# Five layer norms taken apart into blocks inside the neighbouring stages, with the root by Newton steps on VectorE

## The chip, the cores and the metric
The kernel runs on one core of one Trainium2 chip. The time is the device time of one execution in microseconds (us), lower is better.

## What is computed
The input x has 8 sequences of 256 tokens and 128 features. Five stages are added to it one after another, each behind a layer norm without scale and shift; the last two kinds of stage share their weights between calls.

```python
def _layernorm(x, axis=-1, eps=1e-05):
    m = jnp.mean(x, axis=axis, keepdims=True)
    v = jnp.var(x, axis=axis, keepdims=True)
    return (x - m) / jnp.sqrt(v + eps)
...
    x = x + 0.5 * _L0_ffn_ref(_layernorm(x, axis=-1), ...)    # mixture: router, 8 experts, top 2, and a shared one
    x = x + _L0_attn_ref(_layernorm(x, axis=-1), ...)         # four blocks of linear attention and MLP
    x = x + 0.5 * _L0_ffn_ref(_layernorm(x, axis=-1), ...)
    x = x + 0.5 * _L1_ffn_ref(_layernorm(x, axis=-1), ...)    # experts with a capacity: each takes its top 32 tokens of a sequence
    x = x + _L1_attn_ref(_layernorm(x, axis=-1), ...)         # causal attention, 16 heads of 8
    x = x + 0.5 * _L1_ffn_ref(_layernorm(x, axis=-1), ...)
    return x
```

## The kernel before
The state xr lies in SBUF with features on the 128 partitions and the 2048 tokens along the free axis, in four blocks (tb 0 to 3) of 512 tokens. The order on each engine is the order of the code; semaphores counted up by the producers tie the engines together. The stages are ffn0(0), attn0, ffn0(1), ffn1(0), attn1, ffn1(1).

A layer norm stands ahead of every stage but attn0, whose own first norm is part of its periods. It treats all four blocks at once between two stages (norm_parts, on TensorE from L479, on ScalarE from L1002, layer_norm and layer_norm_whole on VectorE from L1326). Per block: TensorE multiplies by the centring matrix into a PSUM bank (xc, L487), ScalarE squares (sq, L1005), TensorE averages over the partitions by a matrix of 1/128, so that each variance stands on all 128 partitions (var, L493), ScalarE takes Ln (L1009). When all four are done it loads another table and takes Exp of -0.5 times that (L1013), VectorE multiplies (L1329 or L1345). For three of the norms the result is also split into a rounded high half by ScalarE (high, L1017) and a low half by VectorE (low, L1334). Matmuls in which accuracy matters are made three times with these halves (mm3, L122 to L124).

The mixture, ffn0, has 72 units n. Unit n is up(n) on TensorE (six matmuls), gate(n) on ScalarE (silu), product(n) on VectorE, weigh(n) by the router's weight from unit 8 on, high(n) on ScalarE, the low half on GpSimd (L1800), and down(n) on TensorE four units later (LAG0). up(n) waits for product(n-2). Ahead of it stand the router's logits, 16 matmuls of 8 columns (L517). On VectorE, best() finds the two largest, places() their indices, choose() makes the weights; a DMA through DRAM spreads them. In the first call VectorE also splits four experts' weights between the products (split), and GpSimd four more (L1804). add(tb) adds a finished block to xr.

attn0 runs in 20 periods (PERIODS); period p works on block p mod 4 in its newest role and on three older roles. The last three periods only drain. In each, ScalarE's last gelu is fed (L1133), on which VectorE's residual2 (L1509) waits; behind that TensorE centres (L573), and so on to finish (L1513), which adds the block to xr.

ffn1 scores the tokens (L667), turns z (L672), picks 32 tokens per expert by eight rounds of max on VectorE, gathers, multiplies in 32 steps g, and at the end turns the outputs back (outputs), scales them by their gate on ScalarE (gated) and scatters them with one-hot matrices (scatter); add(tb) adds a block when two sequences are scattered. attn1 begins with project_in of block 0 in two halves (quad 0 and 1), each of four mm3; ScalarE (hm, L1248) and VectorE (stk, L1689) stack the results, and then the heads' scores follow (plain, L814). Its last steps are outputs, flip, normalise, turn, project_out and add.

## Time and profile before
| | us |
|---|---|
| median of 3 runs | 1147.11 |
| lowest and highest | 1139.55, 1149.39 |
| profiled execution | 1144.14 |
| its span | 1142.4 |
| TensorE, VectorE, ScalarE, GpSimd busy | 954.2, 672.9, 626.3, 349.1 |

The span is the part of the profiled execution in which instructions ran. Busy times overlap. In the rows below an engine's name is short: PE is TensorE, PEld its weight loads, DVE VectorE, ACT ScalarE, POOL GpSimd. A matmul of fp32 stands as two records, one of the halves as one.

### The profile page before, as it was taken

What the parts mean: (1) busy time and instruction counts of PE and PEld (TensorE: products, weight loads), DVE (VectorE), ACT (ScalarE), POOL (GpSimd) and SP (SyncE); (2) the same over time, 40 slices, a digit from 0 to 9 for tenths busy, and PEclk for the clock granted to TensorE, in tenths of its full rate; (3) what the DMA queues carried; (4) which work ended last, traced back from release to release, by engine and by line L of the source; (5) the groups of instructions that cost most, each with busy time, mean ns of one, the idle gap of its engine ahead of it and who ended that gap; (6) DMA issues with size and microseconds to landing.
All of it is one profiled execution on the core that took longest, in us unless ns stands there. A gap on an engine that the chain in (4) does not pass through costs nothing.

```text
span 1142.4 us, 12658 instructions
## 1 busy us (share of the span) xinstructions
PE 954.2 (84%) x4387; PEld 637.8 (56%) x4395; DVE 672.9 (59%) x1247; ACT 626.3 (55%) x986; POOL 349.1 (31%) x257
## 2 busy tenths in 40 slices
PE   6899997599999998689999974998567777675998
PEld 4678884233333333257888852886344554443797
DVE  2888885567777877437888826242645545226222
ACT  5455554378888887645555554445342544443443
...
DMA packets 30932, 33.61 MB, mean 29 GB/s; under 512 B 2254, under 2 KB 19990, under 8 KB 30870
## 3 DMA queue, kind: packets, MB, share of 16 engines
...
q14 instruction: 27, 0.22, 0.1%
...
## 4 chain that ended last, share of the span: by engine, by line
PE 63%; DVE 20%; ACT 10%; POOL 3%; issue 3%; DMA 0%; SPq 0%; ACTq 0%; DVEq 0%; POOLq 0%
PE ps L122 10%; PE ps L123 9%; PE ps L124 9%; PE ps L595 5%; PE ps L732 5%; DVE smax L1697 3%; PE ps L753 2%; PE ps L589 2%; PE ps L814 2%; PE ps L487 2%; PE ps L573 2%; ACT L1139 2%; ACT ex L1258 2%; PE ps L493 2%; PE ps L704 2%
## 5 line engine op out<-in xcount | busy, mean ns | idle before, releaser
L1800 POOL TENSOR_TENSOR fl<-fp,fh 128x512 fp32r<-128x512 f32 x144 | 225.6, 1588 | 128.5 <-ACT fh L1062 128.4
L1053 ACT ACTIVATE fs<-ps 128x512 f32<-128x512 f32 x144 | 86.2, 599 | 115.6 <-PE ps L124 115.3
L1396 DVE TENSOR_TENSOR fp<-fp,cwb 128x512 f32<-128x512 f32 x128 | 139.0, 1086 | 13.7 <-DVE fp L1389 0.5
L1389 DVE TENSOR_TENSOR fp<-fs,ps 128x512 f32<-128x512 f32 x144 | 98.1, 682 | 38.8 <-ACT fs L1053 37.6
L122 PE MATMUL ps<-z_hi,w_hi 128*128 128x512 f32 x288 | 116.7, 405 | 3.4 <-DVE fp L1389 3.3
L123 PE MATMUL ps<-z_lo,w_hi 128*128 128x512 f32 x288 | 115.7, 402 | 0.0
L124 PE MATMUL ps<-z_hi,w_lo 128*128 128x512 f32 x288 | 114.1, 396 | 0.0
L1062 ACT CAST fh<-fp 128x512 fp32r<-128x512 f32 x144 | 88.8, 617 | 34.7 <-DVE fp L1396 30.2
L1865 POOL TENSOR_TENSOR ln_sq<-ln_rs 128x512 f32<-128x512 f32 x20 | 21.1, 1056 | 272.8 <-ACT ln_rs L1102 272.8
L1858 POOL TENSOR_SCALAR_AFFINE_SELECT ex<-ex 128x1024 f32<-128x1024 f32 (+1 forms) x24 | 33.7, 1403 | 171.8 <-ACT ex L1258 171.8
L1697 DVE TENSOR_REDUCE smax<-ps 128x8 f32<-128x2048 f32 (+1 forms) x24 | 55.0, 2291 | 34.0 <-PE ps L828 27.3
L814 PE MATMUL ps<-stk 32*128 32x128 f32 (+1 forms) x512 | 34.3, 384 | 41.3 <-DVE smax L1697 15.6
L1198 ACT ACTIVATE hid<-ps 128x512 f32<-128x512 f32 x64 | 38.5, 601 | 52.8 <-PE ps L124 52.6
L122 PEld LDWEIGHTS ps<-z_hi,w_hi 128*128 128x128 f32 x288 | 55.6, 193 | 18.6 <-DVE fp L1389 5.9
L732 PE MATMUL ps<-hid,w 128*128 128x256 f32 x256 | 65.2, 379 | 0.0
L589 PE MATMUL ps<-z,wb 128*128 128x512 f32 x128 | 62.4, 614 | 2.7 <-DVE qq L1472 2.7
L124 PEld LDWEIGHTS ps<-z_hi,w_lo 128*128 128x128 f32 x288 | 55.5, 193 | 12.7
L122 PE MATMUL ps<-fh,w_hi 128*128 128x512 f32 x144 | 57.3, 398 | 5.8 <-POOL fl L1800 5.8
L123 PEld LDWEIGHTS ps<-z_lo,w_hi 128*128 128x128 f32 x288 | 55.7, 193 | 10.9
L1258 ACT ACTIVATE ex<-ps 128x2048 f32<-128x2048 f32 x24 | 44.8, 1872 | 29.1 <-PE ps L814 29.1
L595 PE MATMUL ps<-hid,wb 128*128 128x512 f32 x128 | 60.2, 593 | 0.0
L581 PE MATMUL ps<-z,wb 128*128 128x512 f32 x96 | 49.6, 657 | 10.7 <-DVE z L1447 10.7
...
## 6 DMA issues: line engine op xcount, KB each, us to landing
...
stk<-mT SPq DMA_DIRECT2D x64, 4.0 KB
```

The lines of the kernel that those rows point to most:

```text
L122: pe.matmul(out, w_hi, x_hi, start=start, stop=False)
L123: pe.matmul(out, w_hi, x_lo, start=False, stop=False)
L124: return pe.matmul(out, w_lo, x_hi, start=False, stop=stop)
L589: pe.matmul(ps[:, bank, :], wb[:, b, (4 + k) * P:(5 + k) * P], blk(z, t), start=True, stop=True).then_inc(a0_matmul[t], 1)
L595: pe.matmul(ps[:, A0_WO, :], wb[:, b, w], hid[:, k, :], start=(k == 0), stop=(k == FT - 1)).then_inc(a0_matmul[t], 1)
L732: ins = pe.matmul(ps[:, OUT1[n % 2], 0:SEQ], w2[:, e, ft * P:(ft + 1) * P], hid[:, g % RING1, f * SEQ:(f + 1) * SEQ], start=(ft == 0), sto ...
L1053: act.activation(fs[:, n % 2, :], ps[:, n % 2, :], ACT.Silu).then_inc(silu_done, 1)
L1062: act.copy(fh[:, n % RING0, :], fp[:, n % RING0, :]).then_inc(fhi_done, 1)
L1389: dve.tensor_tensor(f, fs[:, n % 2, :], ps[:, 2 + n % 2, :], ALU.mult).then_inc(prod_done, 1)
L1396: dve.tensor_tensor(f, f, cwb[:, x % CW_RING, :], ALU.mult).then_inc(weighed, 1)
L1697: dve.tensor_reduce(smax[:, s % 2, int(k > 0), :, hgs], ps[:, bank:bank + 4, :].rearrange("p g (h t) -> p g h t", h=HG if k == 0 else 2), ...
L1800: pool.tensor_tensor(fl[:, n % RING0, :], fp[:, n % RING0, :], f32(fh[:, n % RING0, :]), ALU.subtract).then_inc(flo_done, 1)
```

## The change
The norm is cut into six steps that are each called for one block: ln_centre, ln_variance and ln_spread on TensorE, ln_square and ln_high on ScalarE, ln_root, ln_scale and ln_low on VectorE. The old norm_parts, layer_norm and layer_norm_whole and the Ln and Exp with their table loads are gone. ln_square also copies the centred block to z, since the bank is written again. ln_variance has the squares as weights and one column of 1/128 as the moving side, so that each token's variance comes out once, in four columns on the partitions. ln_root makes the reciprocal root there, on 128x4 values: a seed by integer arithmetic and three Newton steps. ln_spread multiplies the identity by one column repeated 128 times, which puts the root of each token on every partition again. ln_scale multiplies that with z.

New steps on TensorE, with the banks:

```diff
-LG_BANK, CW_BANK = OUT0[0], OUT0[3]
+LG_BANK, CW_BANK = OUT0[1], OUT0[3]
...
+LN_BANK = {LN_FFN0: (4, 5, 6, 7), LN_FFN0B: (5, 5, 6, 7), LN_FFN1: OUT0, LN_ATTN1: (0, 1, 6, 7), LN_FFN1B: (0, 1, 3, 5)}
...
+def ln_centre(n, tb):
+    pe.wait_ge(ln_in, NTB * n + tb + 1)
+    pe.matmul(ps[:, LN_BANK[n][tb], :], centre[:], blk(xr, tb), start=True, stop=True).then_inc(xc_ready, 1)
+def ln_variance(n, tb):
+    pe.wait_ge(sq_ready, 2 * (NTB * n + tb + 1))
+    for q in range(TPB):
+        ins = pe.matmul(ps[:, LN_BANK[n][tb], q:q + 1], LN_SQ[n][:, tb, q * P:(q + 1) * P], mean_w[:, 0:1], start=True, stop=True)
+    ins.then_inc(var_ready, 1)
...
+def ln_spread(n, tb):
+    pe.wait_ge(rs_ready, NTB * n + tb + 1)
+    for q in range(TPB):
+        ins = pe.matmul(ps[:, LN_BANK[n][tb], q * P:(q + 1) * P], ln_r[:, tb, q:q + 1].broadcast_to([P, P]), ident[:],
+                        start=True, stop=True)
+    ins.then_inc(spread_ready, 1)
```

On ScalarE:

```diff
+def ln_square(n, tb):
+    act.wait_ge(xc_ready, NTB * n + tb + 1)
+    act.activation(LN_SQ[n][:, tb, :], ps[:, LN_BANK[n][tb], :], ACT.Square).then_inc(sq_ready, 1)
+    act.copy(blk(z, tb), ps[:, LN_BANK[n][tb], :]).then_inc(sq_ready, 1)
...
+def ln_high(n, tb):
+    act.wait_ge(y_done, NTB * HALVED.index(n) + tb + 1)
+    act.copy(blk(z_hi, tb), blk(z, tb)).then_inc(zh_done, 1)
```

On VectorE:

```diff
+def ln_root(n, first, last=None):
+    last = first if last is None else last
+    v, r, t = (x[:, first:last + 1, :] for x in (ln_v, ln_r, ln_t))
+    for tb in range(first, last + 1):
+        dve.wait_ge(var_ready, NTB * n + tb + 1)
+        own.did(dve.tensor_scalar(ln_v[:, tb, :], ps[:, LN_BANK[n][tb], 0:TPB], EPS_OUT, None, ALU.add))
+    own.wait()
+    own.did(dve.tensor_scalar(r.bitcast(I32), v.bitcast(I32), -0.5, ROOT_SEED, ALU.mult, ALU.add))
+    own.wait()
+    for step in range(ROOT_STEPS):
+        own.did(dve.tensor_tensor(t, r, r, ALU.mult))
+        own.wait()
+        own.did(dve.scalar_tensor_tensor(out=t, in0=t, scalar=-0.5, in1=v, op0=ALU.mult, op1=ALU.mult))
+        own.wait()
+        ins = dve.scalar_tensor_tensor(out=r, in0=t, scalar=1.5, in1=r, op0=ALU.add, op1=ALU.mult)
+        if step < ROOT_STEPS - 1:
+            own.did(ins)
+            own.wait()
+    ins.then_inc(rs_ready, last + 1 - first)
+def ln_scale(n, tb):
+    done = y_done if n in HALVED else z_ready
+    dve.wait_ge(spread_ready, NTB * n + tb + 1)
```

Where they are called. The start, on TensorE and then on VectorE:

```diff
+ln_centre(LN_FFN0, 1)
+ln_variance(LN_FFN0, 0)
+ln_centre(LN_FFN0, 2)
+ln_variance(LN_FFN0, 1)
+ln_spread(LN_FFN0, 0)
+ln_spread(LN_FFN0, 1)
+ln_variance(LN_FFN0, 2)
+ln_spread(LN_FFN0, 2)
 pe.wait_ge(par_loaded, 16 * (len(PAR_NAMES) + 6))
...
 dve.tensor_scalar(centre[:], ident[:], -1.0 / P, None, ALU.add).then_inc(centre_ready, 1)
 own.did(dve.tensor_copy(ident_b[:], ident[:]))
+ln_root(LN_FFN0, 0, 1)
+ln_scale(LN_FFN0, 0)
...
 dve.wait_ge(w0_loaded[0], 16 * W0_LOADS[0])
 halves(w0_hi[:, 0, :], w0_lo[:, 0, :], w0_raw[:, 0, :]).then_inc(w0_split, 1)
+ln_low(LN_FFN0, 0)
```

The mixture, on TensorE, ScalarE and VectorE; the norm of ffn1(0) begins inside the second call:

```diff
+    pe.wait_ge(z_ready, u0 + 1)
+    up(0)
+    ln_centre(ln, NTB - 1)
+    up(1)
+    logits(1)
     logits(0)
-    up(0)
-    for tb in range(1, NTB):
-        logits(tb)
-    for n in range(1, ALL0):
+    ln_variance(ln, NTB - 1)
+    logits(2)
+    up(2)
+    ln_spread(ln, NTB - 1)
+    up(3)
+    logits(3)
+    for n in range(4, ALL0):
         up(n)
-        if n >= LAG0:
-            down(n - LAG0)
...
+        down(n - LAG0)
+        if n == LAG0 + 2:
             weights()
+        if call == 1:
+            for tb in range(NTB - 1):
+                if n == LAST0[tb] + 8:
+                    ln_centre(LN_FFN1, tb)
+                if n == LAST0[tb] + 10:
+                    ln_variance(LN_FFN1, tb)
+                if n == LAST0[tb] + 13:
+                    ln_spread(LN_FFN1, tb)
+                if n == LAST0[tb] + 16:
+                    scores(LN_FFN1, tb)
     for n in range(ALL0 - LAG0, ALL0):
         down(n)
+    if call == 1:
+        ln_centre(LN_FFN1, NTB - 1)
+        ln_variance(LN_FFN1, NTB - 1)
+        ln_spread(LN_FFN1, NTB - 1)
+        scores(LN_FFN1, NTB - 1)
...
+            ln_square(ln, NTB - 1)
+            ln_high(ln, 2)
         if n >= 1:
             high(n - 1)
-        if n == LAG0 + 1:
+        if n == 3:
+            ln_high(ln, NTB - 1)
+            weigh_two()
+        if n == LAG0 + 2:
             weights()
...
+    ln_low(ln, 2)
     product(0)
+    ln_root(ln, NTB - 1)
+    product(1)
+    ln_scale(ln, NTB - 1)
+    product(2)
+    ln_low(ln, NTB - 1)
     best()
...
+        if call == 1 and n - 11 in LAST0[:NTB - 1]:
+            ln_root(LN_FFN1, LAST0.index(n - 11))
+        if call == 1 and n - 14 in LAST0[:NTB - 1]:
+            ln_scale(LN_FFN1, LAST0.index(n - 14))
```

The last periods of attn0 on TensorE, ScalarE and VectorE:

```diff
+        if period == PERIODS - 1:
+            ln_variance(LN_FFN0B, 1)
...
             pe.wait_ge(a0_vector[tp], V0("m2", bp - 1))
+        if period == PERIODS - 1:
+            ln_centre(LN_FFN0B, 2)
         variance(ta, A0_VAR, 2, ba - 1)
+        if period == PERIODS - 3:
+            pe.wait_ge(a0_vector[rc[0]], V0("vv1", rc[1]))
+            ln_centre(LN_FFN0B, 0)
+        if period == PERIODS - 2:
+            ln_spread(LN_FFN0B, 0)
+        if period == PERIODS - 1:
+            ln_spread(LN_FFN0B, 1)
+            ln_variance(LN_FFN0B, 2)
+            ln_spread(LN_FFN0B, 2)
         if rc:
             project(*rc)
         if rd:
...
+        if period == PERIODS - 3:
+            ln_variance(LN_FFN0B, 0)
+        if period == PERIODS - 2:
+            pe.wait_ge(y_done, NTB * HALVED.index(LN_FFN0B) + 1)
+            ln_centre(LN_FFN0B, 1)
...
+        if period == PERIODS - 3:
+            ln_square(LN_FFN0B, 0)
+        if period == PERIODS - 2:
+            ln_high(LN_FFN0B, 0)
+            ln_square(LN_FFN0B, 1)
+    ln_square(LN_FFN0B, 2)
+    ln_high(LN_FFN0B, 1)
...
+        if period == PERIODS - 2:
+            ln_scale(LN_FFN0B, 0)
         normal2(ta, ba - 1)
         if ba == NBLK:
             finish(ta)
+        if period == PERIODS - 3:
+            ln_root(LN_FFN0B, 0)
+        if period == PERIODS - 2:
+            ln_low(LN_FFN0B, 0)
+            ln_root(LN_FFN0B, 1)
+    ln_scale(LN_FFN0B, 1)
+    ln_root(LN_FFN0B, 2)
+    ln_low(LN_FFN0B, 1)
+    ln_scale(LN_FFN0B, 2)
```

The end of the first ffn1 into attn1, TensorE and then VectorE. ScalarE takes ln_square(0), ln_square(1), ln_high(0) and ln_high(1) one behind each of gated(4) to gated(7); blocks 2 and 3 follow at the head of attn1:

```diff
             scatter(n - 1)
+        if call == 0:
+            if n == HALF1:
+                ln_centre(LN_ATTN1, 0)
+            if n == HALF1 + 1:
+                ln_variance(LN_ATTN1, 0)
+                ln_centre(LN_ATTN1, 1)
+            if n == HALF1 + 2:
+                ln_spread(LN_ATTN1, 0)
+                ln_variance(LN_ATTN1, 1)
+            if n == HALF1 + 3:
+                ln_spread(LN_ATTN1, 1)
+                ln_centre(LN_ATTN1, 2)
...
-    pe.wait_ge(cmask_done, 1)
-    pe.wait_ge(z_ready, u0 + 1)
+    ln_variance(LN_ATTN1, 2)
+    ln_centre(LN_ATTN1, 3)
+    ln_spread(LN_ATTN1, 2)
+    pe.wait_ge(z_ready, u0 + 2)
     project_in(0, 0)
+    ln_variance(LN_ATTN1, 3)
+    ln_spread(LN_ATTN1, 3)
     pe.wait_ge(z_ready, u0 + NTB)
...
+    ln_root(LN_ATTN1, 0)
+    ln_root(LN_ATTN1, 1)
+    ln_scale(LN_ATTN1, 0)
+    add(2)
+    ln_scale(LN_ATTN1, 1)
+    ln_low(LN_ATTN1, 0)
+    add(3)
+    ln_root(LN_ATTN1, 2)
+    ln_low(LN_ATTN1, 1)
+    ln_scale(LN_ATTN1, 2)
+    ln_root(LN_ATTN1, 3)
+    ln_low(LN_ATTN1, 2)
+    ln_scale(LN_ATTN1, 3)
 def attn1():
-    layer_norm(NTB * LN_ATTN1)
     def normalise(s):
```

The end of attn1, TensorE and then VectorE. ScalarE squares blocks 0 and 1 at the end of s = 7, block 2 ahead of and block 3 behind its last turn:

```diff
                 project_out(tb - 1)
+        if s == SEQS - 1:
+            ln_centre(LN_FFN1B, 0)
+            ln_centre(LN_FFN1B, 1)
+            ln_variance(LN_FFN1B, 0)
+            ln_variance(LN_FFN1B, 1)
+    ln_spread(LN_FFN1B, 0)
+    ln_spread(LN_FFN1B, 1)
+    ln_centre(LN_FFN1B, 2)
     turn(NTB - 1)
+    ln_variance(LN_FFN1B, 2)
+    pe.wait_ge(z_ready, NTB * LN_FFN1B + 2)
     project_out(NTB - 1)
+    ln_spread(LN_FFN1B, 2)
+    ln_centre(LN_FFN1B, 3)
+    ln_variance(LN_FFN1B, 3)
+    for tb in range(NTB - 1):
+        scores(LN_FFN1B, tb)
...
                 add(tb - 1)
+        if s == SEQS - 1:
+            ln_root(LN_FFN1B, 0, 1)
+            ln_scale(LN_FFN1B, 0)
+            ln_scale(LN_FFN1B, 1)
+    ln_root(LN_FFN1B, 2)
     low(NTB - 1)
     add(NTB - 1)
+    ln_scale(LN_FFN1B, 2)
+    ln_root(LN_FFN1B, 3)
```

The order of the instructions at two places. First VectorE in the last periods of the first attention. res is what residual2 and residual1 write, fo comes from fed. Before:

```order
L1439 SCALAR_TENSOR_TENSOR ln_sq<-ps,eps,ln_sq 128x512 [waits a0_square1]
L1505 TENSOR_TENSOR res<-a_104,z 128x512 [waits a0_scalar3]
L1444 SCALAR_TENSOR_TENSOR ln_rs<-ln_sq,ln_rs 128x512 [waits a0_vector1]
L1447 SCALAR_TENSOR_TENSOR z<-ps,ln_rs 128x512 [waits a0_vector1]
L1454 TENSOR_SCALAR z<-z,par 128x512 [waits a0_vector1]
L1513 TENSOR_TENSOR xr<-xr,z 128x512 [waits a0_vector1]
L1509 TENSOR_TENSOR res<-fo,z 128x512 [waits a0_scalar2]
L1431 TENSOR_TENSOR z<-ps,ln_rs 128x512 [waits a0_scalar3]
```

And now:

```order
L1606 TENSOR_TENSOR xr<-xr,z 128x512 [waits a0_vector1]
L1403 TENSOR_SCALAR ln_v<-ps 128x4 [waits var_ready]
L1405 TENSOR_SCALAR ln_r<-ln_v 128x4 [waits dve_step]
L1408 TENSOR_TENSOR ln_t<-ln_r 128x4 [waits dve_step]
L1410 SCALAR_TENSOR_TENSOR ln_t<-ln_t,ln_v 128x4 [waits dve_step]
L1412 SCALAR_TENSOR_TENSOR ln_r<-ln_t,ln_r 128x4 [waits dve_step]
...
L1412 SCALAR_TENSOR_TENSOR ln_r<-ln_t,ln_r 128x4 [waits dve_step]
L1602 TENSOR_TENSOR res<-fo,z 128x512 [waits a0_scalar2]
L1524 TENSOR_TENSOR z<-ps,ln_rs 128x512 [waits a0_scalar3]
L1526 TENSOR_SCALAR z<-z,par 128x512 [waits a0_vector3]
```

What moved: behind the add to xr of block 1 the eleven operations of the first root, waiting for var_ready, stand ahead of residual2.

Second, VectorE at the head of the second mixture. fp is what product writes, lg the logits, mx and ix their maxima and indices. Before:

```order
L1334 TENSOR_TENSOR z_lo<-z,z_hi 128x512 [waits zh_done]
L1389 TENSOR_TENSOR fp<-fs,ps 128x512 [waits silu_done]
L1355 TENSOR_TENSOR lg<-ps,bias_e 128x128 [waits lg_ready]
L1359 MAX mx<-lg 128x8 [waits dve_step]
L1359 MAX mx<-lg 128x8 x15
L1361 TENSOR_TENSOR e_80<-mx 128x16 [waits dve_step]
L1389 TENSOR_TENSOR fp<-fs,ps 128x512 [waits silu_done]
L1365 MAX_INDEX ix<-mx,lg 128x8 x8
L1389 TENSOR_TENSOR fp<-fs,ps 128x512 [waits silu_done]
L1365 MAX_INDEX ix<-mx,lg 128x8 x8
L1389 TENSOR_TENSOR fp<-fs,ps 128x512 [waits silu_done]
```

And now:

```order
L1425 TENSOR_TENSOR z_lo<-z,z_hi 128x512 [waits zh_done]
L1469 TENSOR_TENSOR fp<-fs,ps 128x512 [waits silu_done]
L1403 TENSOR_SCALAR ln_v<-ps 128x4 [waits var_ready]
L1405 TENSOR_SCALAR ln_r<-ln_v 128x4 [waits dve_step]
L1408 TENSOR_TENSOR ln_t<-ln_r 128x4 [waits dve_step]
L1410 SCALAR_TENSOR_TENSOR ln_t<-ln_t,ln_v 128x4 [waits dve_step]
...
L1469 TENSOR_TENSOR fp<-fs,ps 128x512 [waits silu_done]
L1421 TENSOR_TENSOR z<-ps,z 128x512 [waits spread_ready]
L1469 TENSOR_TENSOR fp<-fs,ps 128x512 [waits silu_done]
L1425 TENSOR_TENSOR z_lo<-z,z_hi 128x512 [waits zh_done]
L1435 TENSOR_TENSOR lg<-ps,bias_e 128x128 [waits lg_ready]
```

What moved: a low half stands ahead of the first product, the root of block 3 ahead of the second, and the maxima stand behind the third product where they stood behind the first.

## Rows read from the trace of the kernel before

**Rows 1.** The chain of waits on the page: shares of the span by engine.
```profile
PE 63%; DVE 20%; ACT 10%; POOL 3%; issue 3%; DMA 0%; SPq 0%; ACTq 0%; DVEq 0%; POOLq 0%
```

**Rows 2.** Table by stage; first line gives the columns.
```profile
core 0: us, PE busy (x) PEld busy (x) DVE busy (x) ACT busy (x) POOL busy (x), PEclk, DMA share, GB/s
22.50:33.00 10.50, 10.50 (x38) 9.34 (x39) 3.79 (x22) 2.50 (x3) 0.00 (x0) 0.50 0.00 0
502.00:524.00 22.00, 20.89 (x76) 17.04 (x77) 12.65 (x67) 8.61 (x16) 6.39 (x5) 0.72 0.54 147
524.00:660.00 136.00, 135.93 (x593) 110.94 (x592) 113.20 (x133) 76.05 (x132) 104.09 (x67) 1.00 0.22 63
660.00:681.00 21.00, 15.75 (x56) 10.61 (x57) 4.13 (x7) 10.51 (x15) 1.43 (x2) 0.85 0.00 1
1013.00:1031.00 18.00, 14.55 (x50) 9.05 (x50) 3.39 (x6) 8.61 (x13) 0.00 (x0) 0.78 0.00 0
```

**Rows 3.** Timeline, second layer norm: start, length, engine, line, instruction.
```profile
485.68 0.69 DVE L1513 TENSOR_TENSOR xr<-xr,z 128x512 f32<-128x512 f32 x1
487.98 0.60 ACT L1005 ACTIVATE ln_sq<-ps 128x512 f32<-128x512 f32 x1 [4.97 <-PE ps L487]
496.13 1.28 ACT L1031 ACT_TABLE_LOAD   x1
497.42 1.15 ACT L1013 ACTIVATE ln_rs<-ln_rs 128x512 f32<-128x512 f32 x2
...
502.01 0.77 PE L122 MATMUL ps<-z_hi,w_hi 128*128 128x512 f32 x1
504.71 5.12 PE L517 MATMUL ps<-par,z 128*128 128x8 f32 x24
```

**Rows 4.** Timeline of VectorE: small operations that depend on one another.
```profile
682.08 0.25 DVE L1544 RECIPROCAL scr<-scs 128x16 f32<-128x16 f32 x1
...
821.34 0.18 DVE L1704 TENSOR_SCALAR mneg_r<-smax 128x32 fp32r<-128x32 f32 x1
821.55 0.18 DVE L1707 COPY mneg<-mneg_r 128x32 f32<-128x32 f32 x1
```

**Rows 5.** Timeline of TensorE: eight transposes in the experts' tail.
```profile
779.54 1.04 PE L743 MATMUL ps<-ident,yt 128*128 128x128 f32 x8
```

**Rows 6.** Timeline: centres and first unit of the start, products behind choose().
```profile
7.72 2.63 PE L487 MATMUL ps<-xr,centre 128*128 128x512 f32 x4
22.51 0.77 PE L122 MATMUL ps<-z_hi,w_hi 128*128 128x512 f32 x1
...
41.30 0.67 DVE L1389 TENSOR_TENSOR fp<-fs,ps 128x512 f32<-128x512 f32 x1
...
521.38 1.26 DVE L1389 TENSOR_TENSOR fp<-fs,ps 128x512 f32<-128x512 f32 x2
523.80 0.60 ACT L1053 ACTIVATE fs<-ps 128x512 f32<-128x512 f32 x1 [0.93 <-PE ps L124]
```

**Rows 7.** Timeline, last periods of the first attention.
```profile
463.53 0.69 ACT L1133 ACTIVATE fo<-ps,par 128x512 f32<-128x512 f32 x1 [1.12 <-PE ps L595]
464.25 0.69 DVE L1509 TENSOR_TENSOR res<-fo,z 128x512 f32<-128x512 f32 x1 [2.10 <-ACT fo L1133]
...
468.44 3.60 PE L589 MATMUL ps<-z,wb 128*128 128x512 f32 x8
```

**Rows 8.** Timeline, end of the second mixture: last add, reduction of the scores.
```profile
663.76 0.69 DVE L1400 SCALAR_TENSOR_TENSOR xr<-ps,xr 128x512 f32<-128x512 f32 x1 [3.04 <-PE ps L124]
...
680.76 0.29 DVE L1538 TENSOR_REDUCE scm<-ps 128x16 f32<-128x128 f32 x1 [4.79 <-PE ps L667]
```

**Rows 9.** Timeline from the experts into the second attention.
```profile
789.46 0.69 DVE L1628 TENSOR_TENSOR xr<-ps,xr 128x512 f32<-128x512 f32 x1 [3.20 <-PE ps L753]
...
801.48 0.77 PE L122 MATMUL ps<-z_hi,wst_hi 128*128 128x512 f32 x1 [4.99 <-DVE z_lo L1334]
...
811.08 0.60 PE L814 MATMUL ps<-stk 32*128 32x256 f32 x8 [2.44 <-DVE stk L1689]
```

**Rows 10.** Timeline behind the second attention: reduction of the scores.
```profile
1030.80 0.29 DVE L1538 TENSOR_REDUCE scm<-ps 128x16 f32<-128x128 f32 x1 [4.06 <-PE ps L667]
```

196 lines of the change are left out of this document (77 added, 119 removed).

## The prediction, made before the changed kernel ran
> **What bounds the kernel now.** I read the chain of waits first, then a table by stage, then the timeline around each of the five layer norms. The chain shows who sets the end: TensorE has 63% of it, VectorE 20%, ScalarE 10% [rows 1]. So what counts is time in which TensorE stands still or runs at half clock, and work that is added to it where it is full. The table by stage shows both kinds. From 524 to 660 us, the second mixture of experts (called the mixture from here), TensorE is busy 135.93 of 136 us at clock 1.00: there every added matmul costs its whole length. In the 10.5 us behind the first layer norm the clock is 0.50, in the 22 us behind the second 0.72, and 0.85 and 0.78 in the stretches of the third and fifth [rows 2]. The timeline of the second norm shows what a norm of all four blocks costs: the last residual add runs from 485.68 to 486.37, ScalarE loads a table at 496.13 and begins its first Exp at 497.42, and the first up-projection starts at 502.01, 15.6 us behind the add. Then come 24 records of router logits [rows 3].
>
> **What the edits are and what one block costs.** Removed per block: a Ln (0.69) and an Exp (0.6) on ScalarE, and per norm two table loads of 1.28 us. Kept: centre, square, scale, split. Added:
> - A root on VectorE: one read of PSUM, one seed and nine dependent operations, 11 in a row, each waiting for the one before. Rows of before show such a chain: a 128x32 operation at 821.34 and the one that depends on it at 821.55 [rows 4], so 0.21 apart, 2.35 us in all. From below 11 times 0.17 (nothing less than 0.16 shows in such rows), from above 11 times the reciprocal at 682.08 with the same hand-over, 0.29 [rows 4]: 1.9 to 3.2. I take 2.35, since the operations are of the kind at 821.
> - A copy of the centred block on ScalarE, the size of the square (0.60, [rows 3]), and the variance waits for both: 1.2 us where 0.6 stood.
> - The variance by four matmuls with the squares as weights. They are the same shape of work as the router logits, 24 records in 5.12 us at half clock [rows 3], so 1.7 us a block there and 0.85 at full: no cheaper than the 0.86 of the 512-column matmul.
> - A spread by four matmuls of 128 columns, 8 records: eight records of 128 columns took 1.04 us with their tail at 779.54 [rows 5], 0.86 start to start; 1.7 at half clock. Bounds 0.8 to 1.7.
> So a block has 2.6 us on TensorE at full clock in place of 1.7, and the chain from the residual add to the scaled block is 0.9 + 1.2 + 0.9 + 2.35 + 0.9 + 0.7, with hand-overs 7.2 us. One block's tail in place of four is the gain; that every root stands in VectorE's own queue, ahead of work that TensorE waits for, is the price. I work out five places.
>
> **A. The start, +11 us (9.5 to 14).** TensorE centres from 7.72, as before. The square and copy of block 1 end near 12.0, its variance at 13.5, the joint root of blocks 0 and 1 (12 operations, 2.5) at 16.1. Then VectorE does in order: scale 0 and 1 (to 18.6, behind two spreads), root 2 (2.4, to 21.2), the split of the first weights (1.5), low halves 0 and 1 (1.4), scale 2 (0.7), the parameter copies (0.6): 25.5. TensorE waits for those copies ahead of its first up-projection, so this starts at 25.5 to 27.3 where it was 22.51 [rows 6]: +3 to +4.8. Behind it the router comes later: block 3 is centred behind up(0); its root (2.4) stands ahead of product(1), which up(3) waits for; its logits come behind up(3), gate(3), the high copy and the low half. By adding these up (up 1.4 at full and 2.6 at half clock) best() starts 17 to 20 us behind up(0), and choose() ends 26 to 29 us behind it. Before, the product behind choose() started at 41.30, 18.8 behind up(0) [rows 6]. Behind choose() VectorE's chain of four weight splits and products is the same less one product (-0.6). Sum 3.6 + 27 - 18.8 - 0.6 = 11.2. Nothing absorbs it: the splits follow one another on VectorE and GpSimd.
>
> **B. End of the first attention and second mixture, +6.5 us (3.5 to 11).** In period 17 TensorE gets centre(0) ahead of project (+0.9 to 1.7, it is busy from there). ScalarE squares and copies block 0 behind fed (ended 464.22), TensorE makes the variance, VectorE the root, and all of this stands ahead of residual2 of block 2, which before started at 464.25, 0.03 behind fed [rows 7]. It now starts 4.6 later; 0.7 of that was slack, the spread adds 0.9: the up-projections at 468.44 [rows 7] move by 4.6. In period 18 the same stands ahead of residual2(3), with the high copy: 0.6 + 1.2 + 0.1 + 0.9 + 2.4 = 5.2. The last add so ends 10.7 to 13 later, near 498. Scale 1, root 2 and spread 2 (4.1 to 5) stand ahead of up(0), which starts at 501.3 to 505, against 502.01 [rows 3]: 12 us of gap are gone and 11 come back inside the attention. Then the router's order as in A: choose() ends 26 to 29 behind up(0) where it was 19.4 (521.38, [rows 6]). Unit 6 had its silu at 523.80 [rows 6] and unit 7 one period of about 2.06 later (nine matmuls of the mixture, 136 us for 66 units in [rows 2]), 23.9 behind up(0); now unit 7 comes at 28.3 to 31.3: +4.4 to +7.4. Sum, middle: 0.5 + 6.
>
> **C. Second mixture into the capacity experts, +5 us (2.5 to 8).** Blocks 0 to 2 bring centre, variance, spread and scores, 4 x 0.86 = 3.44 us each, into a TensorE that is full [rows 2]: +10.3. VectorE gets 3.1 us each (root and scale); it has 113.2 of 136 us busy, so the sum fits, but the root in one piece delays the product that up(n+2) waits for by 2.4, against a slack of 1.2: up to 1.2 each, in part under the centre and variance put in ahead. I take 0.7 each, 2. At the end block 3 alone has the chain: add ends 664.45 [rows 8], then 7.2, then scores 0.9 to 1.7: the reduction of the scores starts near 673.5 where it was 680.76 [rows 8]: -7.2 (6.3 to 8). Sum 10.3 + 2 - 7.2.
>
> **D. Into the second attention, +6 us (5 to 7.5).** High(0) on ScalarE waits for scale(0), which VectorE has behind root(0) and root(1); gated(7), which the last scatter waits for, stands behind high(0). So the last add moves from 790.15 to near 796.5. The first project_in starts near 800.1 (before 801.48, [rows 9]). But VectorE's first stack operation stands behind root(3) and scale(3): root(3) ends near 806.2, spread 807.1, scale 807.8; the four stack steps take 3.3, then low(3), and only then project_in(0,1): 811.7. Four more stack steps end at 816.5. The scores of the heads start there in place of 811.08 [rows 9]: +5.4.
>
> **E. Out of the second attention, +4 us (0 to 9).** Two centres and two variances stand ahead of the last sequence's outputs, and VectorE has its joint root and two scales (waiting for spreads that TensorE issues behind flip(7)) ahead of normalise(7). Adding up: outputs end 1010.5 to 1012.5, normalise(7) 1016 to 1019, root 2 1020 to 1023, project_out 1021.5, block 3 behind it 7.2 and the scores; the reduction starts at 1030.7 at full clock throughout, up to 1040 at half. Before 1030.80 [rows 10]. This stretch ran at 0.78 [rows 2]; I take 4.
>
> **Sum.** 11 + 6.5 + 5 + 6 + 4 = +32.5 us. The profiled execution took 1144.14 (span 1142.4), so it would be 1176.6; the median of the runs lies 3.0 above it, so 1147.1 + 32.5 = 1179.6, say 1179. All ends together give 20.5 to 49.5.
>
> The removed table loads are costed by rows: a load is 1.28 us, and the Exp behind the one at 496.13 starts at 497.42, 0.01 later [rows 3]. The Trainium skill (ScalarE: Activation LUTs, "What ACT_TABLE_LOAD costs") adds a drain of about 1.38 us to each, 2.66 in all. By that the five loads on the path would give back 6.9 us more, and the sum would be 25.6. The trace does not agree: no such gap stands behind the load.
>
> **The rivals.**
> 1. Faster: VectorE's queue hides the roots, because what stands behind each was early. Then the transitions keep their gain: B -12 (gap 15.6 becomes 4), D -7, E -7, C +3, A 0: -23, 1124 us. For it speak the gaps and the idle of VectorE, busy 12.65 of the 22 us behind the second norm and 4.13 of the 21 us around the third [rows 2]. Against it: residual2 started 0.03 us behind its input, so nothing was early there [rows 7]. It decides from a slack of about 4 us ahead of each root.
> 2. Clock: TensorE no longer stands still at the transitions and keeps 2.4 GHz. By the clocks in [rows 2] the four stretches would give back 5.2, 6.2, 3.2 and 4.0, 18.6; about 5 is in my ends already, so -13: 1166. Against: TensorE still waits 3 to 5 us for roots, and the logits alone did not raise the clock (24 records at half in [rows 3]).
>  The Trainium skill (TensorE: Matmul & The Clock Gate, "Part 1: The HAM clock gate") says that activity releases the throttle and idling brings it back; by that rule the price is as in rival 2 where the new order leaves no gap, and nothing where it does.
> 3. No measurable change: the stalls in A and B are half as long since units catch up behind them, and C's woven work costs 7: sum near +6, 1153. Against: the mixture has no idle to catch up with [rows 2].
> 4. Longer: a spread from a repeated column and a root at their upper ends, stalls in every unit: 1205.
>
> **How the numbers follow.** Forecast 0.62; rival 1 0.11; rival 2 0.13; rival 3 0.09; rival 4 0.05. A measurement of this kernel tells about 1% from no change, 11.5 us. Slower by more: 0.62 + 0.13 + 0.05 = 0.80; within 1%: 0.09; faster 0.11. The range leaves out rival 1 and rival 4 and ends at the sum's upper end: 1150 to 1198.
>
> **What would show it.** Right: the root group at 2.2 to 2.6 us, residual2 in the last two periods more than 4 us behind fed, the first up-projection at 25 to 27 us, choose() ending 26 or more behind up(0), TensorE's busy time in the second mixture up by 10, head scores starting 5 later behind the last add of the experts. Wrong: up(0) of the second mixture before 498, best() within 12 us of up(0), or a clock of 1.00 in the 20 us behind each norm.

## The result and the profile after

The changed kernel takes 1189.73 us (median of 4 runs, 1187.85 to 1191.39) against 1147.61 us before (4 runs, 1139.55 to 1149.39): 1.038 times as long, 95% interval 1.033 to 1.043. The forecast was 1179 with a range of 1150 to 1198, so direction and range held; the measured time is 10.7 us above the forecast. The profiled execution took 1191.39 us with a span of 1189.7, 47.3 us more than the span of before. The medians are 42.1 us apart; the places below are read from the profiles and so add up to the larger number, against 32.5 in the forecast's sum.

First the page of the changed kernel: busy time of the engines, the granted clock in 40 slices, and the chain of waits by engine.

```profile
PE 987.2 (83%) x4667; PEld 674.9 (57%) x4675; DVE 707.0 (59%) x1447; ACT 600.6 (50%) x958; POOL 344.9 (29%) x257
...
PEclk7899999789999999779999986999657978775999
...
PE 52%; DVE 19%; POOL 11%; ACT 9%; issue 8%; DMA 1%; SPq 0%; POOLq 0%; ACTq 0%; DVEq 0%
```

TensorE has 33.0 us more to do than before (987.2 against 954.2) in 4667 instructions in place of 4387. Yet its share of the chain fell from 63% to 52% [rows 1]: VectorE has 19%, GpSimd 11%. GpSimd's part is the low half of the products in the mixtures. The next table answers to [rows 2]: the first 10.5 us behind the first up-projection, the head of the second mixture, its full part, the tail behind its last add, and the way out of the second attention.

```profile
core 0: us, PE busy (x) PEld busy (x) DVE busy (x) ACT busy (x) POOL busy (x), PEclk, DMA share, GB/s
28.10:38.60 10.50, 10.49 (x52) 8.46 (x52) 3.12 (x9) 3.31 (x6) 1.27 (x1) 0.80 0.01 2
518.00:545.00 27.00, 23.91 (x104) 19.52 (x103) 14.87 (x79) 8.96 (x18) 6.48 (x5) 0.77 0.33 101
545.00:694.00 149.00, 145.17 (x652) 117.05 (x651) 120.28 (x165) 77.73 (x137) 97.89 (x64) 1.00 0.22 61
701.00:713.00 12.00, 7.04 (x29) 5.67 (x29) 3.44 (x14) 1.07 (x2) 0.00 (x0) 0.65 0.00 0
1045.00:1079.00 34.00, 27.26 (x184) 23.36 (x184) 10.98 (x44) 4.82 (x8) 0.00 (x0) 0.70 0.00 1
```

In the second mixture TensorE is busy 145.17 of 149 us; before it was 135.93 of 136. In the tail it runs at 0.65 of full clock, at the end of the second attention at 0.70; before had 0.85 and 0.78 there [rows 2], in stretches of other lengths (0.83 from the last add to the reduction, and 0.78 also over the 34 us up to the second reduction). In the 22 us behind the first up-projection of either mixture it did not fall: 0.83 against 0.76, and 0.73 against 0.72. Where the time was lost is best read from landmarks that both kernels have. The table gives how much later each comes than in the profile of before; the steps are the losses of my five places.

| landmark (its start before, us) | changed kernel | step | forecast | without Newton steps | step | step with six |
|---|---|---|---|---|---|---|
| silu of unit 71, first mixture (183.89) | +13.1 | A 13.1 | 11 | +13.0 | 13.0 | 18.7 |
| silu of unit 8, second mixture (527.92) | +20.9 | B 7.7 | 6.5 | +14.9 | 1.9 | 15.8 |
| reduction of the scores (680.76) | +32.0 | C 11.1 | 5 | +19.1 | 4.1 | 23.1 |
| first maximum of the second attention (812.69) | +40.9 | D 9.0 | 6 | +22.0 | 3.0 | 17.7 |
| second reduction of the scores (1030.80) | +47.6 | E 6.6 | 4 | +28.8 | 6.8 | 5.4 |

The last three columns are two of the experiments below; the changed kernel has three Newton steps in each root.

All five places lose, each more than I had put down. Three readings show how. The end of the first attention, which answers to [rows 7], by the timeline (start, length, engine, line, instruction, idle time ahead and its releaser):

```profile
477.23 0.69 ACT L1183 ACTIVATE fo<-ps,par 128x512 f32<-128x512 f32 x1 [1.12 <-PE ps L618]
...
480.45 0.16 DVE L1403 TENSOR_SCALAR ln_v<-ps 128x4 f32<-128x4 f32 x1 [4.60 <-PE ps L493]
...
482.42 0.16 DVE L1412 SCALAR_TENSOR_TENSOR ln_r<-ln_t,ln_r 128x4 f32<-128x4 f32 x1
482.50 0.68 DVE L1602 TENSOR_TENSOR res<-fo,z 128x512 f32<-128x512 f32 x1
...
483.33 1.19 PE L596 MATMUL ps<-res,centre 128*128 128x512 f32 x1 [1.01 <-DVE res L1602]
```

fed ends at 477.92. residual2 stands behind eleven root operations, the last one at 482.42, and starts at 482.50, 4.58 us behind fed; before it was 0.03. Of these 2.5 us are VectorE's wait for the variance and 2.1 the root. In the period after it starts 4.81 behind. Now the second mixture, one of three woven roots (L1408 to L1412), what GpSimd does meanwhile, and what TensorE waits for:

```profile
608.10 0.17 DVE L1405 TENSOR_SCALAR ln_r<-ln_v 128x4 int32<-128x4 int32 x1
...
608.73 1.29 POOL L1931 TENSOR_TENSOR fl<-fp,fh 128x512 fp32r<-128x512 f32 x1 [1.28 <-ACT fh L1103]
...
608.89 1.14 DVE L1408 TENSOR_TENSOR ln_t<-ln_r 128x4 f32<-128x4 f32 x1
...
610.06 0.16 DVE L1410 SCALAR_TENSOR_TENSOR ln_t<-ln_t,ln_v 128x4 f32<-128x4 f32 x1
...
610.85 0.16 DVE L1412 SCALAR_TENSOR_TENSOR ln_r<-ln_t,ln_r 128x4 f32<-128x4 f32 x1
610.93 0.69 DVE L1469 TENSOR_TENSOR fp<-fs,ps 128x512 f32<-128x512 f32 x1
...
611.07 1.16 PE L500 MATMUL ps<-ident,ln_r 128*128 128x128 f32 x8 [1.25 <-DVE ln_r L1412]
```

One operation of the root takes 1.14 us in place of 0.16. It ends at 610.03, when GpSimd's low half (608.73 and 1.29 long) ends at 610.02. The same happens to all three roots here (1.14, 1.15, 1.15). So the root takes 3.1 us, the product of the next unit starts at its end, and TensorE stands still for 1.25 us ahead of the spread. The Trainium skill (Trainium Architecture — The Big Picture, "What this means for kernel authors") calls the port pair that VectorE and GpSimd share an exclusive lock and not a bandwidth split; the two end times agree with it. Last the tail of that mixture, against [rows 8], on TensorE:

```profile
701.95 1.12 PE L487 MATMUL ps<-xr,centre 128*128 128x512 f32 x2 [0.78 <-DVE xr L1480]
704.24 1.49 PE L493 MATMUL ps<-mean_w,ln_sq 128*128 128x1 f32 x8 [1.16 <-ACT z L1079]
707.96 2.08 PE L500 MATMUL ps<-ident,ln_r 128*128 128x128 f32 x8 [2.23 <-DVE ln_r L1412]
710.82 1.88 PE L507 MATMUL ps<-par,z 128*128 128x8 f32 x8 [0.78 <-DVE z L1421]
712.55 1.74 PE L707 MATMUL ps<-ident,z 128*128 128x128 f32 x7
```

From the last add (701.20) to the reduction (712.74) it takes 11.5 us where it was 17.0, so 5.5 are gained, not 7.2. The spread takes 2.08 and the scores 1.88 us; at full clock they take 1.16 and 1.06 (the run with unused matmuls, below).

### The profile page after: what moved, and what is told of

The parts are those of the page before. It is cut to its first block, busy times and chain, and to the rows that moved or that the text cites. A ratio compares the mean times of both kernels' runs of the same rounds, so it can differ in the third digit from the quotient of the medians.

```text
span 1189.7 us, 13372 instructions
## 1 busy us (share of the span) xinstructions
PE 987.2 (83%) x4667; PEld 674.9 (57%) x4675; DVE 707.0 (59%) x1447; ACT 600.6 (50%) x958; POOL 344.9 (29%) x257
## 4 chain that ended last, share of the span: by engine, by line
PE 52%; DVE 19%; POOL 11%; ACT 9%; issue 8%; DMA 1%; SPq 0%; POOLq 0%; ACTq 0%; DVEq 0%
POOL fl L1931 10%; PE ps L122 6%; PE ps L123 6%; PE ps L124 6%; PE ps L618 5%; PE ps L767 5%; DVE smax L1816 3%; PE ps L788 2%; PE ps L612 2%; PE ps L860 2%; PE ps L596 2%; PE ps L500 2%; PE ps L487 2%; ACT ex L1321 2%; ACT L1189 2%
## 5 line engine op out<-in xcount | busy, mean ns | idle before, releaser
L1931 POOL TENSOR_TENSOR fl<-fp,fh 128x512 fp32r<-128x512 f32 x144 | 221.1, 1549 | 156.3 <-ACT fh L1103 156.0
L122 PE MATMUL ps<-z_hi,w_hi 128*128 128x512 f32 x288 | 120.4, 418 | 3.7 <-DVE fp L1469 2.6
L122 PEld LDWEIGHTS ps<-z_hi,w_hi 128*128 128x128 f32 x288 | 55.9, 194 | 18.9 <-DVE fp L1469 3.4
L124 PEld LDWEIGHTS ps<-z_hi,w_lo 128*128 128x128 f32 x288 | 56.1, 195 | 13.1
L604 PE MATMUL ps<-z,wb 128*128 128x512 f32 x96 | 49.3, 654 | 10.7 <-DVE z L1540 10.7
```

The costliest lines, as they stand in the source:

```text
L122: pe.matmul(out, w_hi, x_hi, start=start, stop=False)
L124: return pe.matmul(out, w_lo, x_hi, start=False, stop=stop)
L1931: pool.tensor_tensor(fl[:, n % RING0, :], fp[:, n % RING0, :], f32(fh[:, n % RING0, :]), ALU.subtract).then_inc(flo_done, 1)
```

## The experiments

My theory, called Q in the expectations: the roots stand in VectorE's queue on the path to the end. The rival W: the added TensorE work and its half clock carry the loss. Ratios are to the kernel before on the same chip; places are read by the landmarks, against the profile of before. The changed kernel, unaltered, stood beside three of the runs as an anchor.

**The anchor.**

> The changed kernel itself, unaltered, on the chip of the next three runs: the anchor that they are compared with. 36 to 44 us above before; if the root theory's places hold, the same +13, +8, +11, +9 and +7 by stage within 1 us each.

Measured: 1196.34 us, 1.043 times before (1.039 to 1.048). By stage: 13.6, 8.4, 11.0, 9.1 and 10.8. The first four repeat within 0.7; the fifth is 4.2 longer, with 6 more up to the last outputs and 2 fewer behind them. 2.8 of the 6 stand ahead of the two centres that the change put there; the rest is the variances and the outputs of the last sequence (L902) behind them. First the changed kernel, then the same kernel again:

```profile
1045.36 2.42 PE L493 MATMUL ps<-mean_w,ln_sq 128*128 128x1 f32 x16
1047.72 0.66 PE L902 MATMUL ps<-ex,vaug 128*32 128x256 f32 x8
...
1050.12 0.47 PE L905 MATMUL ps<-ex,vaug 128*32 128x128 f32 x8
```

```profile
1049.31 3.41 PE L493 MATMUL ps<-mean_w,ln_sq 128*128 128x1 f32 x16
1052.65 1.10 PE L902 MATMUL ps<-ex,vaug 128*32 128x256 f32 x8
...
1057.34 0.43 PE L905 MATMUL ps<-ex,vaug 128*32 128x128 f32 x8
```

The same outputs take 2.9 us at full clock and 5.1 at half, and the variances that they stand behind 2.36 or 3.34. So differences of a few us in E say nothing between single profiles. The start has its own spread: over seven profiles with an unaltered start the first silu comes 2.9 to 5.6 us late, the silu of unit 8 9.3 to 12.1 and that of unit 71, the landmark of A, 11.0 to 13.6.

**The length of the roots.** Two runs, three Newton steps left out, and three more:

```diff
-ROOT_STEPS = 3
+ROOT_STEPS = 0
```

> Leaves out the three Newton steps of every root (the seed alone is used), so the output is a roughly normalised one. The root on VectorE falls from 2.1 us (3.1 us where one operation meets GpSimd in the second mixture) to about 0.4 us, 18 times. Theory Q (the roots stand in VectorE's queue, on the path): the start and the first router give back 5, the end of the first attention and the second norm 7, the mixture 4 and its tail 2, the way into the second attention 4, the way out 4, so 22 to 28 us: about 1164 us. Theory W (the added TensorE work and the half clock carry the loss, the roots are mostly covered): under 10 us, 1180 us or more.

```diff
-ROOT_STEPS = 3
+ROOT_STEPS = 6
```

> Six Newton steps in place of three: every root 1.8 us longer, the result the same within rounding. Theory Q: the same places lose what the run without steps gives back, or a little more since nothing is covered any longer: 22 to 32 us more, about 1216 us. Theory W: under 10 us more, 1200 us or less.

Measured: 1168.23 us without (1.022 times before, 1.019 to 1.026) and 1224.43 with six (1.073, 1.069 to 1.078), on one chip, where before took 1141.41. Between them lie the two results of the changed kernel, 1.038 and 1.043: the steps cost 18 to 24 us, three more 34 to 40. Both of W's bounds (10 us) are broken. For Q the first run is at or below the low end of what I gave and the second above it. The profile of the first is its slowest run, 6.1 us above the median, so its places add up to more than the median shows. Up to the first maximum of the second attention, ahead of E, there are 15 roots; 1.8 us off each is 27, and 18.9 came back, 1.8 us more on each cost 34.3. So a part of the present length is covered and nothing of a longer one is. The table shows where: B, C and D give back 5.8, 7.0 and 6.0, the start nothing (13.1 and 13.0), though with six steps it loses 5.5 more. Even with a root of 0.4 us no place gains on before. In the middle of the second mixture, by the starts of silu, a plain unit takes 2.09 us. A woven block adds 0.86, 0.90, 0.89 and 0.89 to four units without Newton steps; with three the third is 2.4, with six 6.3. The other two blocks have 5.8 and 5.5 there. Here is the wait ahead of the first spread with six; the spread behind it and the next unit's matmuls run at half clock, which makes the loss larger than the 1.8 us of the steps:

```profile
626.26 2.08 PE L500 MATMUL ps<-ident,ln_r 128*128 128x128 f32 x8 [3.05 <-DVE ln_r L1412]
```

So a woven block costs 3.5 us of matmuls and, with three steps, 1.5 of waits.

**The root cut in two.**

```diff
-                        ln_root(LN_FFN1, LAST0.index(n - 11))
+                        ln_root_part(LN_FFN1, LAST0.index(n - 11), 0)
+                    if call == 1 and n - 12 in LAST0[:NTB - 1]:
+                        ln_root_part(LN_FFN1, LAST0.index(n - 12), 1)
```

> In the second mixture alone each woven root is cut in two: read, seed and first step in one unit, the other two steps in the next. Theory Q: the wait of TensorE ahead of each spread (1.25 to 1.29 us, three of them) and the step of 2.5 us in the times of the units there shrink to 1.0; 3 to 4.5 us less in all, 1186 us. Rival (the wait comes from the one operation that takes 1.15 us beside GpSimd, wherever it stands): it stays at 1 us a block, under 1 us gained.

Then the spread at +14 in place of +13 and the scale at n - 15 in place of n - 14 as well:

> The cut root of the run root_pieces (which had cost 3.6 us a block, since the spread stood where it was and TensorE waited 2.8 us for it), now with the spread one unit later on TensorE and the scale one later on VectorE. If the wait is one of latency (the spread stands too close behind the variance), it goes, and of the 5.3 us a block that the woven norm costs 3.7 are left: 4.5 us less than the unaltered kernel. If it is one of VectorE's throughput, it turns up in another place and nothing is gained.

Measured: 1200.77 us (1.054 times before, 1.049 to 1.060), and 1194.31 (1.045, 1.041 to 1.049). The first run met neither of its expectations, a gain of 3 to 4.5 us or one under 1: it lost. The second piece stands behind the product and the weighing of the next unit, TensorE waits 2.81 us for it, and the matmuls behind that wait run at half clock (0.63 us each in place of 0.39): from the silu of unit 28 of the second mixture to the last add it takes 10.3 us more than the changed kernel. In the second run nothing is gained, as its second expectation said. There are two waits a block, for the root and then for the scale:

```profile
609.08 1.16 PE L500 MATMUL ps<-ident,ln_r 128*128 128x128 f32 x8 [0.73 <-DVE ln_r L1431]
...
615.42 0.83 PE L507 MATMUL ps<-par,z 128*128 128x8 f32 x6 [1.00 <-DVE z L1440]
```

An operation of 1.13 us stands in its second piece too, in all three blocks. The same stretch is 3.6 us longer than in the anchor: the wait comes back in two other places. The explanation by latency falls. The one by VectorE's throughput, with the operation that GpSimd holds up, fits; no run took that operation away from GpSimd.

**The root behind residual2.**

```diff
                         residual2(ta, ba - 1)
+                    if period == PERIODS - 2:
+                        ln_root(LN_FFN0B, 0)
+                    if period == PERIODS - 1:
+                        ln_root(LN_FFN0B, 1)
...
-                    if period == PERIODS - 3:
-                        ln_root(LN_FFN0B, 0)
```

> In the last two periods of the first attention VectorE makes the root of blocks 0 and 1 behind residual2 in place of ahead of it. Theory Q: residual2 starts 0.03 to 0.1 us behind fed again (4.6 and 4.8 now); of that 4.5 us come back in the first of the two periods and 2.8 in the second (TensorE has the variance of block 1 ahead there): 7 us less, about 1183 us. Rival (the end of the attention is set by TensorE, which has three centres, variances and spreads more there): the product moves later instead, under 3 us gained.

Measured: 1186.52 us (1.041, 1.035 to 1.047), no difference that these runs can tell. By stage, from the silu of unit 71 to the last add of the attention, 3.5 to 4.1 us are gained over the two profiles of the changed kernel, and 3.1 to 3.8 of them are left at the silu of unit 8. residual2 starts 0.03 us behind fed again, but TensorE then has other work at half clock:

```profile
477.40 0.69 DVE L1602 TENSOR_TENSOR res<-fo,z 128x512 f32<-128x512 f32 x1 [2.10 <-ACT fo L1183]
...
478.38 1.41 PE L493 MATMUL ps<-mean_w,ln_sq 128*128 128x1 f32 x8 [1.74 <-ACT z L1079]
...
479.65 2.05 PE L600 MATMUL ps<-ln_sq,mean_w 128*128 128x512 f32 x2
...
481.50 1.06 PE L596 MATMUL ps<-res,centre 128*128 128x512 f32 x1
```

The centre of the residual starts at 481.50, 3.4 us behind its input. So VectorE's queue in those two periods explains some 3.5 of B's 7.7 us, between the 7 of the theory and the under 3 of the rival. The new variance (L493) and one of the attention's own (L600), both ahead of the centre on TensorE, stand where the rest was expected to come back.

**The order at the router.** Block 3 is centred, squared, rooted and spread ahead of up(0), and logits, best, places and choose follow in the order of before (both calls of ffn0).

> Block 3 is normed ahead of the first up-projection of both mixtures, and the router has its order of before. The first up-projection comes 3 to 5 us later than in the changed kernel, choose() ends 19 us behind it in place of 26: by theory Q 2 to 4 us less a mixture, 6 in all. Rival (the distance up to choose() is made of the same work in either order, only moved ahead): 0 to 2 in all.

Measured: 1192.57 us (1.041, 1.038 to 1.044). In the first mixture the silu of unit 8 comes 10.7 us late, where two runs of the changed kernel gave 12.1 and 10.6: no difference, though the first silu comes 6.5 to 8.1 later. In the second the loss from the last add of the attention to the silu of unit 8 is 5.5 us larger. The rival holds: the work is only moved ahead, and in the second mixture that costs more than it gives.

**The split of the first weights.**

```diff
+            halves(w0_hi[:, 0, :], w0_lo[:, 0, :], w0_raw[:, 0, :]).then_inc(w0_split, 1)
...
             ln_root(LN_FFN0, 0, 1)
...
-            halves(w0_hi[:, 0, :], w0_lo[:, 0, :], w0_raw[:, 0, :]).then_inc(w0_split, 1)
```

> At the start VectorE splits the first weights and reduces the mask ahead of the first roots, in its idle time, in place of behind root 2 (where it now has 1.5 + 0.25 us of them). The first up-projection comes 1.5 to 3 us earlier. By my term A this comes through to choose() and to the end of the mixture, 2 us less in all. Rival (choose() waits for block 3, which is normed behind the up-projections whatever they start at): under 1 us.

Measured: 1188.94 us (1.039, 1.035 to 1.043). The first silu comes 3.0 us late and the silu of unit 8 11.8, both inside the spread of unaltered starts. The rival holds. With the three runs together (no Newton steps, router, weights) none of the roots' steps, the router's order and the weights ahead of up(0) gives back the 9 to 12 us of A when it is taken away alone. The roots are on the path to the first silu, which comes 1.3 us late without Newton steps, but the silu of unit 8 is then 10.1 late all the same. What is left is the chain of the four blocks itself: a copy, a variance, a spread and a scale, each with its hand-over. That it carries A is not shown; I have not taken it apart.

**The third norm taken out of the mixture.** PE, ScalarE and VectorE each do all four blocks behind the last down-projection:

```diff
-                            if n == LAST0[tb] + 8:
-                                ln_centre(LN_FFN1, tb)
...
-                    ln_root(LN_FFN1, NTB - 1)
-                    ln_scale(LN_FFN1, NTB - 1)
+                    ln_root(LN_FFN1, 0, NTB - 1)
+                    for tb in range(NTB):
+                        ln_scale(LN_FFN1, tb)
```

> The third norm alone is taken out of the second mixture: all four blocks behind its last down-projection, with one joint root, one spread and one scale a block. Theory Q/W by stage: the 15.7 us that the woven norm adds inside the mixture go (3 x 3.67 of matmuls, 3 x 1.55 of waits); the tail from the last add to the reduction of the scores grows from 10.9 us to 14 to 18, against 16.3 in before. So 8 to 12 us less than the changed kernel. Rival (the tail grows by as much as the mixture loses, since the same matmuls now run at 1.2 GHz): 0 to 4 us less.

Measured: 1184.52 us (1.036, 1.032 to 1.040). From the silu of unit 8 to the last add the loss is 2.1 us where it was 16.6. But from the add to the reduction it takes 20.0 us, against 11.5 and, in before, 17.0; I had given 14 to 18. Of C's 11.1 us 6.0 are gone, between what the theory (8 to 12) and the rival (0 to 4) gave. In the whole time the interval overlaps that of the changed kernel (1.033 to 1.043), so the gain is read from the profiles.

```profile
688.44 3.63 PE L493 MATMUL ps<-mean_w,ln_sq 128*128 128x1 f32 x32
694.48 6.33 PE L500 MATMUL ps<-ident,ln_r 128*128 128x128 f32 x32 [2.42 <-DVE ln_r L1405]
700.64 4.55 PE L507 MATMUL ps<-par,z 128*128 128x8 f32 x32
705.05 1.31 PE L701 MATMUL ps<-ident,z 128*128 128x128 f32 x5
```

The four variances take 3.6 us, the spreads 6.2 from the first to the scores, the scores 4.4: the spreads at half clock, behind the wait for the joint root. So the rival was right on the mechanism and not on the size. 2.0 of the 6.0 us go again in the experts behind it.

**Unused matmuls in the waits.** `fill(bank, k)` is k times the matmul of the centre into a bank that nobody reads:

```diff
                     ln_centre(LN_FFN1, NTB - 1)
+                    fill(0, 2)
                     ln_variance(LN_FFN1, NTB - 1)
+                    fill(0, 2)
                     ln_spread(LN_FFN1, NTB - 1)
+                    fill(0, 1)
```

> Unused matmuls (512 columns, 0.86 us each at full clock) are put where TensorE waits: 5 at the end of the second mixture, 6 at the head of the second attention, 5 at its end. They change no result. Clock theory (the loss in these three stretches beyond my terms is the 1.2 GHz clock): the spreads, project_in and scores run at 2.4 GHz, 2, 4 and 4 us come back, 8 to 10 us less than the unaltered kernel. If the waits alone set these stretches: 0 to 3 us more.

Measured: 1182.19 us (1.034, 1.030 to 1.037), against 1.043 for the same kernel without on the same chip: the intervals are apart. By stage against that anchor: 1.8 us less in the tail, 1.6 in the experts, 3.1 at the head of the second attention, 2.1 behind its last outputs. (The anchor's slow stretch up to those outputs, 6.7 us longer, is left out.) TensorE in the tail (L506 is the unused matmul):

```profile
702.85 0.95 PE L493 MATMUL ps<-mean_w,ln_sq 128*128 128x1 f32 x8
703.66 1.96 PE L506 MATMUL ps<-xr,centre 128*128 128x512 f32 x4
706.02 1.16 PE L500 MATMUL ps<-ident,ln_r 128*128 128x128 f32 x8 [0.40 <-DVE ln_r L1424]
...
707.96 1.06 PE L511 MATMUL ps<-par,z 128*128 128x8 f32 x8
```

The spread takes 1.16 us and the scores 1.06, against 2.08 and 1.88. The clock theory holds, with 8.6 us by places where 8 to 10 were expected; 1.6 of them are in the experts, where nothing was filled.

**Everything together.** start_early, root_behind, unweave, and the fills in and behind the second attention:

> The changed kernel with the edits of start_early, root_behind and unweave, and the unused matmuls of fill in and behind the second attention. If the places are independent the gains add up: 2 + 3 + 10 + 8 = 23 us less than the changed kernel, near 1.025 times before; still slower than before, because with the roots all but taken away the start (+10) and the second mixture and its ends stay longer.

Measured: 1180.98 us (1.032 times before, 1.027 to 1.037), not 1.025. Up to the first maximum of the second attention 11.6 to 12.7 us are gained over the two runs of the changed kernel: root_behind's 4 to 5 and unweave's 5.8 are there, and the fill at the head of the second attention gives 1.7, but the experts ahead of it take 1.9 more, as in unweave alone. Unused matmuls alone gave 1.034, so the four edits together show no more in the whole time than that one.

**The kernel before, with its waits filled.**

```diff
             def layer_norm(u0, src, busy=()):
                 norm_parts(u0, src, busy)[1]()
+                for _ in range(4 if u0 // NTB in (LN_FFN1, LN_FFN1B) else 5):
+                    pe.matmul(ps[:, 1, :], centre[:], blk(xr, 0), start=True, stop=True)
```

> The kernel before with 4 or 5 unused matmuls of 512 columns behind the last variance of each of its five norms, where TensorE waits 3.5 to 4.9 us for the first scaled block; it changes no result. Clock theory: TensorE holds 2.4 GHz over the wait, and what follows (logits 5.1 us at half clock, scores 5 to 7, project_in and the first up-projections) takes half as long, 2 to 3 us a norm: 8 to 12 us less than before, 0.99. Rival (the clock falls for another reason, or the matmuls delay the first real one): 0 to 3 us more.

Measured: 1136.33 us (11 runs) against 1143.04 (16 runs), 0.994 times before, 0.991 to 0.996. It is faster than both kernels, by less than I expected. The granted clock over the whole span is 0.907, where it was 0.894. Around the second norm (L519 are the logits, L511 the unused matmuls):

```profile
498.14 4.45 PE L511 MATMUL ps<-xr,centre 128*128 128x512 f32 x10
503.20 1.06 PE L519 MATMUL ps<-par,z 128*128 128x8 f32 x8 [0.60 <-DVE z_lo L1336]
504.11 0.48 PE L122 MATMUL ps<-z_hi,w_hi 128*128 128x512 f32 x1
...
505.58 2.74 PE L519 MATMUL ps<-par,z 128*128 128x8 f32 x24
```

The 24 records of logits take 2.74 us; before they took 5.12 [rows 3]. From the last add of the attention to the silu of unit 8 6.2 us are gained, in the tail of that mixture 2.7, behind the last outputs of the second attention 2.0, and nothing at its head. 2.0 are lost again in the experts, and the start is 2.4 later; whether that is its spread is not shown.

## Why the prediction was right, and where its terms were off

The direction, the sum's sign in all five places and the range held. The main reason stands as it was put: the roots stand in VectorE's own queue ahead of work that TensorE waits for, and TensorE has more work where it is full. But all five places lost more than their terms, so the sum was too low on one side: 32.5 us against 42.1 by the medians and 47.3 by the profiles. Root: forecast 2.35 us, measured 2.1 (480.45 to 482.58), under the 2.2 to 2.6 named as the sign, and 3.1 beside GpSimd. residual2: forecast 4.6 and 5.2 later, measured 4.58 and 4.81 behind fed. Two more of the signs did not come as named: up(0) at 28.1 in place of 25 to 27, and the heads' scores 2.5 us later behind the last add of the experts (24.16 us behind its start, before 21.62 [rows 9]) in place of 5; by the chain of D itself they would have come 1 us earlier behind it.

- **A**, 11 forecast, 13.1 measured (11.0 to 13.6 over the seven profiles). up(0) came at 28.11, 0.8 behind my upper end; choose() ended 26.0 us behind it (26 to 29 forecast). The size was near, the reason is not shown: my sum had the roots on the path, and without their Newton steps the start gives nothing back. That the size came out may be luck.
- **B**, 6.5 forecast, 7.7 measured, inside its ends. Without Newton steps 1.9 is left, so here the roots carry it. Inside B the last add of the attention comes 14.2 later (10.7 to 13 forecast), up(0) of the mixture 3.0 (0.5 taken), and the router adds 4.8 (6 taken).
- **C**, 5 forecast with 2.5 to 8, 11.1 measured: the term that failed. "The root in one piece delays the product that up(n+2) waits for by 2.4, against a slack of 1.2 [...] I take 0.7 each, 2" was mis-sized: the waits are 1.5 a block, 4.6, and GpSimd's hold of one operation of the root, 1.0 us, stands in each of them. The woven matmuls were 3.53 a block in place of 3.44, 10.6 in all. "-7.2" for the tail was -5.5, since spread and scores ran at half clock. The 1.4 that is left is near what plain units, which take 0.03 us longer (below), would add: 52 of them, 1.6. 10.6 + 4.6 + 1.4 - 5.5 = 11.1.
- **D**, 6 forecast with 5 to 7.5, 9.0 measured. The last add (+6.9 from the reduction on; 6.4 forecast) and root(3) came as worked out. The spread of block 3 ran at half clock, 2.08 us in place of the 0.9 taken, so that the scale, the first stack operation and the second project_in came 1.6 to 1.9 us later than in my chain. project_in then ran at half clock too, and the stack operations of VectorE followed it at one in 1.28 us:

```profile
838.88 2.08 PE L500 MATMUL ps<-ident,ln_r 128*128 128x128 f32 x8 [2.23 <-DVE ln_r L1412]
...
845.32 0.79 PE L122 MATMUL ps<-z_hi,wst_hi 128*128 128x512 f32 x1 [4.37 <-DVE z_lo L1425]
...
845.91 0.63 PE L123 MATMUL ps<-z_lo,wst_hi 128*128 128x512 f32 x1
...
847.81 0.75 DVE L1808 SCALAR_TENSOR_TENSOR stk<-ps,bst,hm 128x512 fp32r<-128x512 f32 x1 [2.55 <-ACT hm L1311]
```

- **E**, 4 forecast with 0 to 9, 6.6 measured, 10.8 in the other profile. Behind the last outputs of the attention it takes 27.8 and 25.9 us, before 24.1 and without Newton steps 23.1. Up to them, from the first maximum on, it takes 195.8 to 203.0 us in the twelve profiles with the norms taken apart (before 194.0), with no relation to the roots' length: 195.8 with six steps, 201.8 with none. So part of the 6.6 may be chance.

Rival 1 (the queue hides the roots) is excluded by 4.58 and 4.81 us at residual2. Rival 2 (the clock gets better) was right that the clock has a price (the fills gave 1.6 to 3.1 us a place) and wrong on the sign where it counted most: the change by itself lowered the clock, 0.83 to 0.65 in the tail and 0.78 to 0.70 at the fifth norm, and left it near what it was or a little higher behind the first up-projections. What TensorE did there: in the tail of before it waited once behind the last add, 3.45 us ahead of the scores; now it waits 0.78, 1.16, 2.23 and 0.78 us ahead of centre, variance, spread and scores. That these waits are the cause is argued from the fills alone. The Trainium skill's rule (TensorE: Matmul & The Clock Gate, "Part 1: The HAM clock gate"), that activity lifts the throttle and idling brings it back, agrees with what the fills did. It speaks for a change only if the new order closes the gaps, and this one put several in the place of one. Rival 3 is excluded by the time. Rival 4 (every unit stalls) by the units between the woven groups, which all take 2.09 us.

What stays open: most of A, and 0.033 us a unit in the mixtures. In the changed kernel, without Newton steps and unwoven a plain unit takes 2.093 us, in before and in before with fills 2.060: nine matmuls of the same work at clock 1.00, each 0.004 longer. Over the two mixtures (126 units behind unit 8 of each) that is near 4 us of the 47. The new small tiles move the addresses of those behind them; that this is the cause was not tried.
